# Ranking the edges of a window: sums of shifted one-hot rows, or a running scan with windows outermost

## The reference, cut to what matters

```
edge_index = jnp.stack([src, dst])
h = jnp.maximum(_layernorm(x, axis=-1), 0.0)
x = x + _L0_gnn_ref(h, edge_index, ...)
h = jnp.maximum(_layernorm(x, axis=-1), 0.0)
x = x + _L1_gnn_ref(h, edge_weight, src, dst, ...)   # weighted means over in- and out-edges, then a gated unit
h = jnp.maximum(_layernorm(x, axis=-1), 0.0)
x = x + _L2_gnn_ref(h, edge_index, edge_attr_4, ...) # kind = argmax of four attributes; four steps of messages
h = jnp.maximum(_layernorm(x, axis=-1), 0.0)
x = x + _L3_gnn_ref(h, edge_index, edge_type_16, ...)
return x
```

## Time and profile before

| what | value |
|---|---|
| time of the profiled execution | 7953.38 us |
| its span, first to last instruction | 7951.6 us |
| PE busy | 5915.1 us (74%) |
| DVE busy | 3612.8 us (45%) |
| ACT busy | 1790.3 us (23%) |
| POOL busy | 2378.7 us (30%) |
| mean granted clock of TensorE | 0.849 |
| first instruction of `sort_bins` on VectorE | 150.40 us |
| first instruction of `decode` | 529.33 us |

### The profile page before, as it was taken

How to read it: one execution, slowest core, us unless ns; L and a number is a source line. 1 busy time by engine, 2 the same in 40 slices (tenths; PEclk the granted TensorE clock), 3 DMA queues, 4 the chain that set the end, 5 groups by cost and what they waited for, 6 DMA issues and landing times. The chain is left out here.

```text
span 7951.6 us, 103414 instructions
## 1 busy us (share of the span) xinstructions
PE 5915.1 (74%) x31740; PEld 4138.0 (52%) x31741; DVE 3612.8 (45%) x8308; ACT 1790.3 (23%) x4498; POOL 2378.7 (30%) x2470
## 2 busy tenths in 40 slices
PE   2557776676676776666668989899898997666665
PEld 1544443566666656666664444444444443665665
DVE  6999998455555545555556532221222214111111
ACT  1016665233333333333331010100101002000000
POOL 0000000566665445655650000000000000666665
PEclk8889999888888888888888999999999998555555
DMA  1015555333333333333335545354453543111111
GB/s 51 1 59 205 206 206 196 105 100 102 102 102 99 83 97 102 103 98 101 101 92 215 198 153 191 128 192 163 156 192 128 191 161 138 45 45 44 46 45 44
DMA packets 418914, 951.22 MB, mean 120 GB/s; under 512 B 61905, under 2 KB 274310, under 8 KB 408582
## 3 DMA queue, kind: packets, MB, share of 16 engines
q1 hardware_dynamic: 314502, 681.10, 25.1%
q0 software_dynamic: 104192, 267.02, 12.5%
HBM read 741.69 MB, written 206.20 MB: 119 GB/s over the span
## 5 line engine op out<-in xcount | busy, mean ns | idle before, releaser
L1518 POOL DMA_INDIRECT ring<-rows,stage x1632 | 1593.5, 976 | 2012.2 <-issue 1040.6
L1589 PE MATMUL ps<-here,spread 128*128 x3264 | 1097.3, 466 | 823.6 <-DVE ring L1548 586.0
L1408 POOL DMA_INDIRECT ring<-rows,stage x808 | 775.5, 960 | 2979.1 <-ACT stage L1392 2579.4
L1168 PE MATMUL ps<-strip,trans_part 128*128 128x512 f16 (+1 forms) x8400 | 1644.2, 357 | 14.2 <-DVE trans_part L1129 14.2
L1168 PEld LDWEIGHTS ps<-strip,trans_part 128*128 128x128 bf16 x8400 | 780.9, 98 | 929.0 <-issue 63.9
L1589 PEld LDWEIGHTS ps<-here,spread 128*128 128x128 f32 x3264 | 656.7, 223 | 948.0 <-issue 878.5
L1548 DVE TENSOR_TENSOR ring<-ring,ps 128x512 f32<-128x512 f32 x816 | 560.6, 687 | 1226.7 <-remote 580.1
L1446 PE MATMUL ps<-ring,mark 128*128 128x128 f32 x1616 | 628.0, 489 | 335.6 <-DMA ring<-rows,stage 248.4
L1607 PE MATMUL ps<-ring,mark 128*128 128x128 f32 x3264 | 769.8, 326 | 0.0
L1607 PEld LDWEIGHTS ps<-ring,mark 128*128 128x128 f32 x3264 | 646.0, 220 | 64.7
L1446 PEld LDWEIGHTS ps<-ring,mark 128*128 128x128 f32 x1616 | 433.2, 326 | 364.5 <-issue 364.3
(11 more groups left out here) (286 smaller groups left out, 6367.3 us busy)
## 6 DMA issues: line engine op xcount, KB each, us to landing
strip<-adj SPq DMA_DIRECT2D x400, 800.0 KB, 4.4
adj<-piece SPq DMA_DIRECT2D x125, 640.0 KB, 3.1
locs<-loc_rows SPq DMA_DIRECT2D x420, 128.0 KB
ahead<-ahead_piece SPq DMA_DIRECT2D x125, 320.0 KB, 2.2
back<-back_piece SPq DMA_DIRECT2D x125, 320.0 KB, 2.4
sheet<-ahead SPq DMA_DIRECT2D x25, 1600.0 KB, 8.6
sheet<-back SPq DMA_DIRECT2D x25, 1600.0 KB, 7.3
ring<-rows,stage POOLq DMA_INDIRECT x2440
```

The lines of the kernel that those rows point to most:

```text
L1168: last = eng.matmul(k.ps[:, b, 0:cols], part[:, s % TABLES, m, t * D:(t + 1) * D], strip[:, n % RING, c0:c0 + cols], start=n == 0 and m == ...
L1408: eng.indirect_dma_start(ring[:, t, :], None, rows, bass.IndirectOffsetOnAxis(stage[:, t:t + 1], 0)).then_inc(s_full[q], 16)
L1518: eng.indirect_dma_start(ring[:, t, :], None, rows, bass.IndirectOffsetOnAxis(stage[:, t:t + 1], 0)).then_inc(s_full[q], 16)
L1589: last = eng.matmul(hid[:, j, :], spread[:, q, t * P:(t + 1) * P], here[:, bass.ds(cols[t] * 2, W2)], start=True, stop=True)
```

## The change

The layout of the counting part is turned: windows of sources outermost, columns innermost (900 numbers, without the padding bin), and the sum over columns is made by a scan instead of shifted matmuls.

- `hot` (L597 after) is now [25, 36]. It is made from every second number of `own_bin` and a table `window` of 900 numbers that GpSimd writes.
- `run` (L603 after) is a `tensor_tensor_scan` over the 900 numbers, with a table `keep` that is 0 at the first column of each bin and 1 elsewhere, so that the running sum starts anew. It takes the place of `twos` and `fours`.
- `hot_j` (L605 after) is a second one-hot tile in the old layout, for the products `word`. `hot_j` and `word` have two buffers each, not three.
- The wait on `s_perm` stands ahead of the scan, and asks for the 72 matmuls of window w-2 in `scan(w)`; it stood ahead of the products and asked for w-3.
- `count(w)` is four matmuls (L648, L649 after) in place of 16. `lower` is the old table less one.
- `rank` (L621 after) reduces `picked` over an axis with a step of 36 numbers. `rank16` (L622 after) is a bf16 copy of it, twice each.
- `place` is made by one instruction for each chunk (L628 after), three for a window, in place of 36.

```diff
-    hot_all = k.sb("hot_row", [P, 3, 1 + J, NS], BF16, own)
-    hot = hot_all[:, :, 1:1 + J, :]
-    twos = k.sb("hot_twos", [P, 2 + J, NS], BF16, own)
-    fours = k.sb("hot_fours", [P, 2, J, NS], BF16, own)
+    window = k.sb("window_no", [P, NW, J], F16, own)
+    window_j = k.sb("window_row", [P, NW + 1], F16, own)
+    hot_j = k.sb("hot_row", [P, 2, J, NW + 1], BF16, own)
...
+    keep = k.sb("keep", [P, NW, J], BF16, own)
+    hot = k.sb("hot", [P, 3, NW, J], BF16, own)
+    run = k.sb("run", [P, 2, NW, J], BF16, own)
...
-    word = k.sb("word", [P, 3, J, WORDS, NS], BF16, own)
+    word = k.sb("word", [P, 2, J, WORDS, NW + 1], BF16, own)
...
+            eng.iota(window[:, :, :], [[1, NW], [0, J]], 0, 0, allow_small_or_imprecise_dtypes=True).then_inc(s_set, 1)
+            eng.iota(window_j[:, :], [[1, NW + 1]], 0, 0, allow_small_or_imprecise_dtypes=True).then_inc(s_set, 1)
             eng.iota(slot_no[:, :], [[1, SLOT]], 0, 0, allow_small_or_imprecise_dtypes=True).then_inc(s_set, 1)
-            eng.memset(hot_all[:, :, 0, :], 0.0).then_inc(s_set, 1)
-            eng.memset(twos[:, 0:2, :], 0.0).then_inc(s_set, 1)
+            eng.memset(keep[:, :, :], 1.0).then_inc(s_set, 1)
+            eng.wait_ge(s_set, 4)
+            eng.memset(keep[:, :, 0:1], 0.0).then_inc(s_set, 1)
...
-                eng.tensor_tensor(in_pairs(hot[:, w % 3, :, :]), every(window_j, J),
-                                  own_bin[:, :, :].unsqueeze(2).to_broadcast([P, J, NS // 2, 2]), ALU.is_equal).then_inc(s_hot, 1)
+                eng.tensor_tensor(hot[:, w % 3, :, :], own_bin[:, :, 0].unsqueeze(1).to_broadcast([P, NW, J]), window[:, :, :],
+                                  ALU.is_equal).then_inc(s_hot, 1)
                 eng.wait_ge(s_hot, w + 1)
-                c.step(eng.tensor_tensor(twos[:, 2:2 + J, :], hot[:, w % 3, :, :], hot_all[:, w % 3, 0:J, :], ALU.add))
                 if w >= 2:
                     eng.wait_ge(s_cnt, w - 1)
-                eng.tensor_tensor(fours[:, w % 2, :, :], twos[:, 2:2 + J, :], twos[:, 0:J, :], ALU.add).then_inc(s_run, 1)
-                if w >= 3:
-
-                    eng.wait_ge(s_perm, CHUNKS * (w - 2))
+                    eng.wait_ge(s_perm, CHUNKS * (w - 1))
+                eng.tensor_tensor_scan(flat(run, w % 2), keep[:, :, :].rearrange("p s j -> p (s j)"),
+                                       flat(hot, w % 3), 0.0, ALU.mult, ALU.add).then_inc(s_run, 1)
+                c.step(eng.tensor_tensor(in_pairs(hot_j[:, w % 2, :, :]), every(window_j, J),
+                                         own_bin[:, :, :].unsqueeze(2).to_broadcast([P, J, (NW + 1) // 2, 2]), ALU.is_equal))
...
-                d.step(eng.tensor_reduce(rank[:, :], picked[:, :, :], AX.X, ALU.add))
+                d.step(eng.tensor_reduce(rank[:, :], picked[:, :, :].rearrange("p s j -> p j s"), AX.X, ALU.add))
+                d.step(eng.tensor_copy(rank16[:, :, :], rank[:, :].unsqueeze(2).to_broadcast([P, J, 2])))
...
-                    for i in range(CH):
-                        j = ch * CH + i
-                        last = eng.tensor_scalar(place[:, n % 3, i, :], slot_no[:, :], rank[:, j:j + 1], None, ALU.is_equal)
-                    last.then_inc(s_place, 1)
+                    eng.tensor_tensor(in_pairs(place[:, n % 3, :, :]), every(slot_no, CH),
+                                      rank16[:, ch * CH:(ch + 1) * CH, :].unsqueeze(2).to_broadcast([P, CH, SLOT // 2, 2]),
+                                      ALU.is_equal).then_inc(s_place, 1)
...
-                    last = eng.matmul(k.psf[:, at + a:at + b], lower[:, :], flat(hot, w % 3)[:, a:b], start=True, stop=False,
-                                      skip_group_check=True)
-                    for gap in range(NS, b, 4 * NS):
-                        lo = max(a, gap)
-                        last = eng.matmul(k.psf[:, at + lo:at + b], all_one[:, :], flat(fours, w % 2)[:, lo - gap:b - gap],
-                                          start=False, stop=gap + 4 * NS >= b, skip_group_check=True)
+                    eng.matmul(k.psf[:, at + a:at + b], all_one[:, :], flat(run, w % 2)[:, a:b], start=True, stop=False)
+                    last = eng.matmul(k.psf[:, at + a:at + b], lower[:, :], flat(hot, w % 3)[:, a:b], start=False, stop=True)
```

More of the change, by code:

```diff
@@ L557, in sort_bins @@
     all_one = k.sb("all_one", [P, P], BF16, own)
-    picked = k.sb("picked", [P, J, NS], F32, own)
+    keep = k.sb("keep", [P, NW, J], BF16, own)
+    hot = k.sb("hot", [P, 3, NW, J], BF16, own)
+    run = k.sb("run", [P, 2, NW, J], BF16, own)
+    picked = k.sb("picked", [P, NW, J], F32, own)
     rank = k.sb("rank", [P, J], F32, own)
+    rank16 = k.sb("rank16", [P, J, 2], BF16, own)
     over = k.sb("over", [P, J], F32, own)
     past = k.sb("past_all", [P, NW], F32, own)
-    word = k.sb("word", [P, 3, J, WORDS, NS], BF16, own)
+    word = k.sb("word", [P, 2, J, WORDS, NW + 1], BF16, own)
     place = k.sb("place_hot", [P, 3, CH, SLOT], BF16, own)
@@ L567, in sort_bins @@
      s_ovs, s_first) = (k.sem(x) for x in names)
-    flat = lambda t, i: t[:, i, :, :].rearrange("p j s -> p (j s)")
+    flat = lambda t, i: t[:, i, :, :].rearrange("p s j -> p (s j)")
+    CHUNKS = J // CH
     PERM = 4
@@ L581, in _ @@
             c = Count(eng, s_first)
-            c.step(eng.tensor_copy(lower[:, :], k.before[:, :]))
+            c.step(eng.tensor_scalar(lower[:, :], k.before[:, :], -1.0, None, ALU.add))
             c.step(eng.memset(all_one[:, :], 1.0))
@@ L593, in scan @@
                     eng.wait_ge(s_cnt, w - 2)
-                eng.tensor_tensor(in_pairs(hot[:, w % 3, :, :]), every(window_j, J),
-                                  own_bin[:, :, :].unsqueeze(2).to_broadcast([P, J, NS // 2, 2]), ALU.is_equal).then_inc(s_hot, 1)
+                eng.tensor_tensor(hot[:, w % 3, :, :], own_bin[:, :, 0].unsqueeze(1).to_broadcast([P, NW, J]), window[:, :, :],
+                                  ALU.is_equal).then_inc(s_hot, 1)
                 eng.wait_ge(s_hot, w + 1)
-                c.step(eng.tensor_tensor(twos[:, 2:2 + J, :], hot[:, w % 3, :, :], hot_all[:, w % 3, 0:J, :], ALU.add))
                 if w >= 2:
                     eng.wait_ge(s_cnt, w - 1)
-                eng.tensor_tensor(fours[:, w % 2, :, :], twos[:, 2:2 + J, :], twos[:, 0:J, :], ALU.add).then_inc(s_run, 1)
-                if w >= 3:
-                    eng.wait_ge(s_perm, CHUNKS * (w - 2))
+                    eng.wait_ge(s_perm, CHUNKS * (w - 1))
[3 more added lines that the diff above has]
+                                         own_bin[:, :, :].unsqueeze(2).to_broadcast([P, J, (NW + 1) // 2, 2]), ALU.is_equal))
                 for a in range(WORDS):
-                    eng.tensor_tensor(in_pairs(word[:, w % 3, :, a, :]), in_pairs(hot[:, w % 3, :, :]),
-                                      words[:, a, bass.ds(first, J), :].unsqueeze(2).to_broadcast([P, J, NS // 2, 2]),
+                    eng.tensor_tensor(in_pairs(word[:, w % 2, :, a, :]), in_pairs(hot_j[:, w % 2, :, :]),
+                                      words[:, a, bass.ds(first, J), :].unsqueeze(2).to_broadcast([P, J, (NW + 1) // 2, 2]),
                                       ALU.mult).then_inc(s_word, 1)
-            eng.wait_ge(s_set, 4)
+            eng.wait_ge(s_set, 5)
             scan(0)
@@ L616, in _ @@
                 q = k.psf[:, (w % 2) * 2 * BANK:(w % 2) * 2 * BANK + F]
-                d.step(eng.tensor_tensor(picked[:, :, :].rearrange("p j s -> p (j s)"), q, flat(hot, w % 3), ALU.mult))
-                d.step(eng.tensor_reduce(rank[:, :], picked[:, :, :], AX.X, ALU.add))
+                d.step(eng.tensor_tensor(picked[:, :, :].rearrange("p s j -> p (s j)"), q, flat(hot, w % 3), ALU.mult))
+                d.step(eng.tensor_reduce(rank[:, :], picked[:, :, :].rearrange("p s j -> p j s"), AX.X, ALU.add))
+                d.step(eng.tensor_copy(rank16[:, :, :], rank[:, :].unsqueeze(2).to_broadcast([P, J, 2])))
                 for ch in range(CHUNKS):
```

12 lines of the change are left out of this document (4 added, 8 removed).

## The result

Four executions of the changed kernel, timed beside the kernel before, have a median of 7998.92 us (7987.53 to 8007.56) against 7945.86 us (7935.0 to 7953.38). The ratio is 1.0067, with a 95% interval of 1.0055 to 1.0081: slower by about 53 us (44 to 64 by the interval). The forecast was 8000 us.

A forecast was written before the change was run, and what follows sets the result against it. VectorE, busy 95% of the loop, was taken as the bound, then a loop through VectorE and TensorE at 16.95 us a window. 7950.5 + 49.5 us lost = 8000 us; 8-in-10 range 7962 to 8038.

The forecast's parts named there:

- Prices: On VectorE, from trace rows: scan 2.03 us, strided reduction 1.74, `hot` 1.10, each `place` instruction 1.75.
- The wait: Ahead of the scan, VectorE waits about 1.3 us a window for the 72 matmuls, taken as 6.3 us.
- The sum: Loop through both engines: 16.95 us a window against 15.00, last matmul 577.0 us against 527.5, 49.5 us lost.
- The start: GpSimd writes `window` and `keep` before the loop: about 1.6 us later, first `own_bin` at 153.2 us.
- The place saving: Three `place` instructions on VectorE take 5.02 us against 7.05, saving 2.03, covered by the wait but for the first chunk.
- The reduction at a step, two rules: For `rank`, one skill rule gives about 1.09 us; the cacheline rule, with L482, supports the 1.74 us taken.
- The rival with a cheap reduction: `rank` not slowed by its step: windows of 16.0 to 16.3 us, 7980 us in all; chance 0.23.
- Two readings that were off without harm: TensorE idles about 7.5 us, not 5, so matmuls start at clock 0.5; VectorE asks for them only two windows later.
- A sign of being wrong that came: Stages behind `decode` differing by more than a few microseconds would show the prediction wrong.

The follow-up runs named there:

- the turned write: Changed kernel with `picked` stored columns outermost, so the product writes at a step and the reduction reads contiguous numbers: 7997.13 us, ratio 1.0071.

## Why the prediction was right, point by point

- **Prices.** The scan was priced by one row of 25 numbers that cost as much as 50: 2.03 us, measured 2.033. The reduction at a step was priced by L482, at a step of 16 bytes: 1.74, measured 1.735. `hot` 1.10 (1.096), `place` 1.75 (1.754). Only the step from `hot_j` to the words was 0.76 us and not 0.68.
- **The wait.** Foreseen at 1.3 us in 23 windows, 30 us; measured 1.43 and 32.8. The 72 matmuls took 6.42 us (6.3 taken), after 7.47 us of idle time (7.5). The later wait gives 31.9 us back, the filled idle time 28.8: both conditions of the wait, its early place and the low clock, are shown.
- **The sum.** A window of 17.07 us (16.95), `decode` at 579.69 (579), 50.4 us lost before it (49.5). The timed runs say 53. That it came so close is in part luck. The 6.3 us were picked between 5.4 and 7.5 us, and a window with another term in it came out at the same 17.07 us. And two small errors cancel: 23 windows of 17.07 are 2.8 us more than 23 of 16.95, while the last 72 matmuls took 4.80 us where 6.3 had been added.
- **The start.** `own_bin` first at 153.3 us (153.2).
- **The place saving, called covered but for its first chunk.** Right: putting the old one back costs 16.8 us of loop, where VectorE's own difference would be 45.
- **The reduction at a step, two rules.** It took 1.735 us read at the step, and the product 1.81 us written at one, against 1.09 without. The Trainium skill, Advanced Engine Details and Errata, "SBUF Cachelines", says that going to a different line with each access is penalised; the trace agrees. The Trainium skill, VectorE: DVE Perf Modes, "Mode 1× (REGULAR) — the baseline", says that the slowest mode takes odd strides at one result a cycle; that does not hold here, and the measurement decides.
- **Where the working was wrong without harm.** The rival with a cheap reduction was priced at 7980 us, "as the clock has less time to fall". Made on the chip, such a reduction left the window at 17.07 us and the ratio at 1.0060. As far as that one run shows, the 0.64 us was a true cost of VectorE and no part of the loss. The sum hid this, since I added the term to a fixed 6.3 us for the matmuls, while these change with what stands around them: 6.42 us in the changed kernel, 7.05 us with the cheap reduction. Of the 50.4 us, the scan is worth 40 in its place, the wait 32, the step 1; these overlap and do not add.
- **Two readings that were off without harm.** The working put the low clock at the start of the matmuls down to an idle time of 7.5 us in place of 5. But the 1800 matmuls took 156.9 us before and 158.4 after, and at equal idle times the 72 of a window took from 5.58 to 7.11 us with the later wait; the rise in idle time is not what made the wait. It also said that nothing on VectorE asks for a window's matmuls before two windows later. In fact `place`, with its ring of three chunks, asks for them one window later (the wait on `s_perm` ahead of each chunk), in both kernels; in neither trace does it have to wait.
- **A sign of being wrong that came.** The stages behind `decode` were to differ by a few microseconds at most; in the profiled execution they took 31 us more. The timed runs, 53 us against 50.4 in the loop, do not bear that out, and what it was in that execution stays open.

## What to carry to other kernels

When an edit makes the engine in front quicker and moves a wait forward at once, price them together: with the new counting, the wait cost 3 us behind a step of 7 us and 33 us behind one of 5 us. Put a wait for a buffer directly ahead of the instruction that writes the buffer, behind all that does not. And where a loop passes through TensorE at a low clock, a term taken off another engine may come back as slower matmuls, as the 0.64 us of the reduction did here; test such a term with the wait out of the way, or with the clock held.

## What the runs showed of the hardware that was not expected

- In three kernels whose VectorE work between waits differs (15.64 us a window in the changed one; 0.64 less with the cheap reduction; the turned write) the window came to the same 17.07 us, and the 72 matmuls settled at 6.41, 7.05 and 6.34 us. Where VectorE waits for them, their time is nearly the same in every window (5.71 us with the old counting and the early wait, or two values by turns without the scan). Where it does not, it wanders, from 5.58 to 7.11 us with the later wait. So the period of such a loop is a joint outcome of the work and of when the clock rises; how the clock comes to settle so is not shown.
- 110 matmuls of no use a window made the changed kernel's loop shorter by 28.8 us: the mean clock in the loop rose from 0.70 to 0.94, and the 72 useful ones went from 6.42 to 4.70 us.
- An f32 stream at a step of 100 or 144 bytes costs about 0.64 to 0.72 us more for 900 numbers, read or written, as much for a number as one at a step of 16 bytes.
